# ScalarE makes the convolutions' last tap from TensorE's bank, VectorE adds the other three

## The reference, cut to what matters

```python
def _causal_dwconv(x, w):
    C, K = w.shape
    xt = jnp.transpose(x, (0, 2, 1))
    out = jax.lax.conv_general_dilated(xt, w[:, None, :], window_strides=(1,), padding=[(K - 1, 0)],
                                       feature_group_count=C, dimension_numbers=('NCH', 'OIH', 'NCH'))
    return jnp.transpose(out, (0, 2, 1))
...
q = silu(silu(_causal_dwconv(h @ Wq.T, conv_q)))
k = silu(silu(_causal_dwconv(h @ Wk.T, conv_k)))
v = silu(silu(_causal_dwconv(h @ Wv.T, conv_v)))
q = _l2norm(q.reshape(B, T, nh, hd))
k = _l2norm(k.reshape(B, T, nh, hd))
...
o, memory_state = _delta_scan(k, q, v, beta)
```

## Time and profile before

| what | us |
|---|---|
| median of 3 runs | 1280.63 |
| lowest and highest of them | 1278.09 and 1340.21 |
| the profiled execution's own time | 1278.25 |
| its span, first to last instruction | 1276.4 |
| TensorE busy | 1060.3 (83%) |
| VectorE busy | 944.5 (74%) |
| ScalarE busy | 497.4 (39%) |

### The profile page before, as it was taken

How to read it: one execution, slowest core, us unless ns; L and a number is a source line. 1 busy time by engine, 2 the same in 40 slices (tenths; PEclk the granted TensorE clock), 3 DMA queues, 4 the chain that set the end, 5 groups by cost and what they waited for, 6 DMA issues and landing times.

```text
span 1276.4 us, 22025 instructions
## 1 busy us (share of the span) xinstructions
PE 1060.3 (83%) x8600; PEld 723.6 (57%) x8600; DVE 944.5 (74%) x2425; ACT 497.4 (39%) x1027; POOL 181.4 (14%) x251
## 2 busy tenths in 40 slices
PE   3699778777988999989988998899989889932587
PEld 2356545455556755766566655675566547721465
DVE  3824268897889788987888788977897789779611
ACT  2044254326443644345432653364335443610122
POOL 2000000130122010401040013100040004003100
PEclk9579879978998999989988999999999989975788
DMA  9724023203420143013311242024201300110000
GB/s 288 141 46 72 10 75 76 41 1 100 77 41 1 50 111 63 1 34 95 76 21 33 76 82 35 1 75 101 48 2 32 88 2 1 34 58 0 16 9 9
DMA packets 93608, 67.69 MB, mean 53 GB/s; under 512 B 47233, under 2 KB 86337, under 8 KB 93505
## 3 DMA queue, kind: packets, MB, share of 16 engines
q1 hardware_dynamic: 88544, 60.75, 20.1%
q10 hardware_dynamic: 4960, 5.54, 1.6%
HBM read 45.55 MB, written 20.32 MB: 52 GB/s over the span
## 4 chain that ended last, share of the span: by engine, by line
PE 41%; DVE 37%; ACT 8%; DMA 4%; issue 4%; SPq 4%; POOL 1%; DVEq 0%; ACTq 0%; POOLq 0%
PE bank L1558 7%; DVE lane_buf L1189 5%; PE bank L1509 4%; PE bank L1538 4%; DVE state L1208 4%; PE bank L1712 4%; DVE state L1201 4%; DVE u_l L1196 4%; PE bank L1655 3%; PE bank L1543 3%; PE bank L1504 3%; DVE lane_buf L339 2%; DMA q_l<-lane_q 2%; PE bank L1450 2%; DVE mx L1005 2%
## 5 line engine op out<-in xcount | busy, mean ns | idle before, releaser
L697 ACT ACTIVATE probs<-bank 128x512 f32<-128x512 f32 x256 | 152.1, 597 | 200.1 <-PE bank L1543 199.7
L1558 PE MATMUL bank<-probs,v_ext 128*9 128x128 f32 x2048 | 162.0, 279 | 12.1 <-ACT probs L697 6.7
L1005 DVE TENSOR_REDUCE mx<-bank 128x2 f32<-128x320 f32 x256 | 120.9, 486 | 54.3 <-PE bank L1509 49.4
L1703 PE MATMUL bank<-feat_c,wgu 128*128 128x256 f32 (+1 forms) x384 | 96.3, 402 | 57.2 <-DVE hid_c L1256 51.6
L339 POOL TENSOR_TENSOR lane_buf<-state,q_l 128x128 f32<-128x128 f32 x128 | 86.4, 704 | 353.9 <-DVEq L1214 353.9
L1189 DVE TENSOR_TENSOR lane_buf<-state,til 128x128 f32<-128x128 f32 x256 | 109.6, 428 | 17.1 <-POOL lane_buf L584 10.2
L1703 PEld LDWEIGHTS bank<-feat_c,wgu 128*128 128x128 f32 (+1 forms) x384 | 71.1, 190 | 78.1 <-DVE hid_c L1256 55.7
L1558 PEld LDWEIGHTS bank<-probs,v_ext 128*9 128x9 f32 x2048 | 83.5, 91 | 55.1 <-issue 20.3
L1504 PE MATMUL bank<-edge_mask,identb 128*128 128x64 bf16 x512 | 63.1, 208 | 49.8 <-DVE mx L1005 37.6
L1538 PE MATMUL bank<-tri_mask,identb 128*128 128x512 bf16 x256 | 102.1, 399 | 0.5 <-DMA q_stack<-m_rows 0.5
L1543 PE MATMUL bank<-q_stack,k_stack 128*128 128x128 bf16 x1024 | 101.8, 223 | 0.0
(11 more groups left out here) (167 smaller groups left out, 1766.1 us busy)
## 6 DMA issues: line engine op xcount, KB each, us to landing
k_pieces<-conv SPq DMA_DIRECT2D x48, 128.0 KB, 2.3
k_stack<-k_pieces SPq DMA_DIRECT2D x32, 192.0 KB
k_stack<-k_pieces SPq DMA_DIRECT2D x32, 128.0 KB
k_l<-lane_k SPq DMA_DIRECT2D x8, 512.0 KB, 3.6
q_l<-lane_q SPq DMA_DIRECT2D x8, 512.0 KB, 5.6
q_pieces<-conv SPq DMA_DIRECT2D x24, 128.0 KB, 2.0
q_stack<-q_pieces SPq DMA_DIRECT2D x32, 96.0 KB
tok<-in_x SPq DMA_DIRECT2D x8, 256.0 KB, 3.2
```

What stands on the lines that cost most here:

```text
L697: act.activation(probs[:, u % 2], score_bank[u % 2][:], ACT.Exp, scale=float(DK) ** -0.5).then_inc(exp_done, 1)
L1005: dve.tensor_reduce(mx[:, g, 2 * v:2 * v + 2], bank[1 + u % 2][:, 0:2 * SPAN].rearrange("p (h k) -> p h k", h=2), AX.X, ALU.max).then_inc( ...
L1558: last = pe.matmul(bank[5][row:row + VE, col:col + W], v_ext[:, b, kb, h, :], probs[:, u % 2, (hp * 2 + kb) * W:(hp * 2 + kb + 1) * W], st ...
L1703: last = pe.matmul(late_bank[i % 2][0:m, g * BT:(g + 1) * BT], wgu[:, k, g * INTER + 128 * i:g * INTER + 128 * i + m], fc[:, k], start=(k ...
```

## The change

`raw_of` on ScalarE first writes the last tap's product into conv, straight from TensorE's bank, as a copy with conv_w's column as its scale, in two halves. Then it copies the bank into raw as before. VectorE's `convolve` starts from that: three multiply-adds for taps 0 to 2, and no multiply. The wait for pieces_out moves from VectorE to ScalarE, which now writes conv first. `keep_taps` gets a wait for VectorE's own last multiply-add, which reads the columns that it overwrites.

```diff
--- before.py
+++ after.py
@@ -759,8 +759,14 @@
                 act.wait_ge(projb_done, n * 4 + 1)
                 act.activation(beta_l[:], bank[4][:, 0:W], ACT.Exp, scale=-1.0).then_inc(beta_exp, 1)
 
-            def raw_of(n, s):
+            def raw_of(n, s, front):
                 act.wait_ge(projb_done, n * 4 + s + 2)
+                if front and s == 0:
+
+                    act.wait_ge(pieces_out, n * 144 + 288)
+                for hh in range(HH):
+                    act.activation(conv[:, s, hh * BT:(hh + 1) * BT], bank[1 + s][:, hh * BT:(hh + 1) * BT], ACT.Copy,
+                                   scale=conv_w[:, s, hh, TAPS - 1:TAPS])
                 for hh in range(HH):
                     last = act.copy(raw[:, s, hh, :, TAPS - 1:],
                                     bank[1 + s][:, hh * BT:(hh + 1) * BT].rearrange("p (b t) -> p b t", b=B))
@@ -860,14 +866,14 @@
                 if tail:
                     norm_c(s)
                 if following:
-                    raw_of(n, 0)
-                    raw_of(n, 1)
+                    raw_of(n, 0, front)
+                    raw_of(n, 1, front)
                     if scan:
                         output_squares(t)
                 if front:
                     max_rows(n + 1, 2)
                 if following:
-                    raw_of(n, 2)
+                    raw_of(n, 2, front)
                 def late(i):
                     if tail:
                         relu_c(s, i)
@@ -1067,27 +1073,22 @@
                     dve.wait_ge(tok_c_ready, n * 2 - 3)
                 subtract_scale(x2(n), z(n), mv, rstd, rstd_ready, n * 2 + 2).then_inc(z_ready, 1)
 
-            def convolve(n, s, front):
+            def convolve(n, s):
                 dve.wait_ge(raw_ready, n * 3 + s + 1)
-                if front and s == 0:
-
-                    dve.wait_ge(pieces_out, n * 144 + 288)
-                for tap in range(TAPS):
+                for tap in range(TAPS - 1):
                     for hh in range(HH):
                         src = raw[:, s, hh, :, tap:tap + W]
                         dst = conv[:, s, hh * BT:(hh + 1) * BT].rearrange("p (b t) -> p b t", b=B)
                         w = conv_w[:, s, hh, tap:tap + 1]
-                        if tap == 0:
-                            last = dve.tensor_scalar(dst, src, w, None, ALU.mult)
-                        else:
-                            last = dve.scalar_tensor_tensor(out=dst, in0=src, scalar=w, in1=dst,
-                                                            op0=ALU.mult, op1=ALU.add)
-                    if tap < TAPS - 1:
+                        last = dve.scalar_tensor_tensor(out=dst, in0=src, scalar=w, in1=dst,
+                                                        op0=ALU.mult, op1=ALU.add)
+                    if tap < TAPS - 2:
                         done(last)
                 last.then_inc(conv_ready, 1)
 
-            def keep_taps():
-
+            def keep_taps(n):
+
+                dve.wait_ge(conv_ready, n * 3 + 3)
                 dve.tensor_copy(raw[:, :, :, :, 0:TAPS - 1].rearrange("p s h b t -> p (s h b) t"),
                                 raw[:, :, :, :, W:W + TAPS - 1].rearrange("p s h b t -> p (s h b) t"))
 
@@ -1347,12 +1348,12 @@
                 if tail:
                     third_apply(s)
                 if following:
-                    convolve(n, 0, front)
-                    convolve(n, 1, front)
+                    convolve(n, 0)
+                    convolve(n, 1)
                     if has_scan:
                         output_norm(t)
-                    convolve(n, 2, front)
-                    keep_taps()
+                    convolve(n, 2)
+                    keep_taps(n)
                 if has_scan:
                     if not following:
                         output_norm(t)
```

## The result

The changed kernel takes 1285.83 us, the median of 20 runs (1279.83 to 1288.5), beside 1278.46 for the kernel before in the same number of runs (1275.27 to 1281.48, but for one of 1340.21 that the comparison, which takes fast runs alone, leaves out). The ratio of the two is 1.005, with a 95% interval of 1.0039 to 1.0061. So it is slower by 5 to 8 us, and that is clear of noise although it is well inside 2%. The forecast was 1288 us, 0.7% slower, in a range of 1278 to 1297.

What follows compares the result with a forecast made beforehand. The chain lies mostly on TensorE and VectorE, but ScalarE's way to feat_c decides. Five full bodies 7.2, n = 7 0.8, n = 0 0.6, n = 1 0.3: 8.9 us over 1278.25 is 1287.2, set to 1288 for the runs' median; range 1278 to 1297.

Steps and rivals of the forecast that it cites:

- VectorE's saved work gives nothing: In n = 2 to 7 the 17.5 us VectorE loses lie beside ScalarE's chain, only widening 1.2 us of slack.
- Price of a scaled copy: ScalarE's 48 added copies from a bank: 0.36 us apart, so 0.72 us for two in each of three groups.
- the 20 to 23 that I named as a sign: Sign of being right: ScalarE's busy time over the whole kernel rises by 20 to 23 us.
- The DMA issue holds ScalarE: Max rows' DMA issue before the third group: ScalarE does nothing else meanwhile, so that group starts at 567.47, not 566.75.
- the rival in which the copies are half hidden: If the DMA issue doesn't hold ScalarE, a full body pays 0.72 us only once: 1283.6 us; chance 0.12.
- Full body's stage, 1.44 us: From the k projection to the late FFN's first tile: second and third groups each add 0.72 us.
- the 1.4 named as a sign: Sign of being right: the late FFN's weight load (L1726) waits for feat_c about 1.4 us longer.
- n = 7 was taken at 0.8: Body n = 7, without a DMA issue: second group adds some 0.05, third counts in full: 0.8 us.
- n = 0 was taken at 0.6 and n = 1 at 0.3: Bodies whose ScalarE waited for VectorE: slower by 0.6 us (0.4 to 1.1) and 0.3 us (-0.4 to +0.9).
- The 1.44 us is carried to the l2 norms, the lane DMAs and the next attention: Behind the late FFN's first tile ScalarE's chain passes the delay on: five full bodies make 7.2 us.
- bodies that keep their length as a sign of being wrong: Sign of being wrong: full bodies keep some 137 us or grow by 0.7 only.
- TensorE's clock as the case of the other side: Hole of some 1.4 us before L1726 lowers TensorE's clock in seven bodies: 12.6 us more, 1299.8; chance 0.06.

Runs made afterwards that it cites:

- the first pair of profiles: One profiled execution each of the kernel before (1278.25 us) and the changed kernel, whose span was 8.1 us longer.
- the second pair: Both kernels profiled once more, unaltered: one execution each, 1289.2 us for the changed kernel and 1277.15 for the one before.
- the copies without the saving: Changed kernel with VectorE doing all four taps again, its first multiply overwriting ScalarE's scaled copies: 1285.72 us, ratio 1.0051 to the kernel before.
- the tap for q alone: Changed kernel with ScalarE's scaled copies only for q; k and v keep VectorE's four taps: 1279.1 us, ratio 1.0006 to the kernel before.
- The late-issue kernel: Changed kernel with ScalarE's issue of the max rows' DMA moved to the body's end: 1282.33 us, ratio 1.0043 to the kernel before.
- the copies made twice: Changed kernel with each scaled copy made a second time, into a free part of hid: 1303.81 us, ratio 1.0196 to the kernel before.
- the saving alone: Last tap's product left out: ScalarE as before, VectorE three multiply-adds as in the changed kernel: 1277.14 us, ratio 0.9991 to the kernel before.

## Why the prediction was right, and where it missed

**VectorE's saved work gives nothing: right.** It was the first step, and two experiments bear it out, by giving the work back and by taking it alone.

**Price of a scaled copy: right.** I took 0.36 us from start to start by the Relu row; it is 0.365 (0.73 for two). ScalarE's busy time rose by 16.0 us, less than the 20 to 23 that I named as a sign, since the 20.2 us of the new line overlap with their neighbours. By the figure that I set beside it from the Trainium skill (ScalarE: Activation LUTs, "What ACT_TABLE_LOAD costs"), 0.40, each group would be 0.07 longer. The page's duration for one such copy, 280 + 0.833 x 256 = 493 ns as an estimate, stands against 472 measured here; the measurement decides.

**The DMA issue holds ScalarE: right.** It rested on 0.04 us between two rows in three bodies, against the releaser that the profile names. In the changed kernel the profile still writes "[0.80 <-PE bank L1656]" at 568.84, though TensorE had been done for 0.8 us, and taking the issue away brought the group back behind TensorE. So the rival in which the copies are half hidden falls.

**Full body's stage, 1.44 us: right,** 1.45 to 1.47. The weight load's wait grew by 1.20, not by the 1.4 named as a sign, as 0.25 us of the delay reaches TensorE before that wait. n = 7 was taken at 0.8. Its third pair of evictions starts 0.80 us behind TensorE's last projection where it was 0.04, so 0.76; TensorE itself was 0.45 us quicker in that body, at another clock, and so only 0.35 shows at the units. n = 0 was taken at 0.6 and n = 1 at 0.3; the profile has 0.37 and 0.74, but TensorE's projections took 0.15 less and 0.57 more there than in the profile before, so these two are settled to half a microsecond only.

**"The 1.44 us is carried to the l2 norms, the lane DMAs and the next attention": right to there, and wrong as a sum of bodies.** This is the step that failed: I let a full body grow by what its stage grows, and so put what TensorE's clock does behind the stage at nothing. The short full bodies of the changed kernel are 136.8 to 137.0 us, against 136.5 to 136.9 before, so they grow by 0.4 at most; the long ones, of 139.5 to 139.8, grow by 2.7 to 3.3. I named bodies that keep their length as a sign of being wrong, and half of the four did. In the first pair of profiles the five full bodies grew by 0.0, 2.7, 3.3, 0.4 and 1.2 us, 7.5 in all where 7.2 was forecast; in the second pair they grew by 4.8. That the sum came out so near is luck.

Where the 1.45 us goes is seen at two places that I followed through the bodies. The last exponential of the attention starts 77.6 to 77.7 us into the body in the kernel before and at 79.1 after (79.4 in n = 4), still 1.5 apart. The output projection of the attention (wo_a) starts at 86.8 to 87.7 before and at 87.2 after (87.5 in n = 4). Between them the time is 8.1 us in each of the bodies n = 2 to 5 of both profiles of the changed kernel, and 9.2 to 10.1 in those of the kernel before. The windows over that place, three bodies of before (n = 2, 3, 4) and two of the changed kernel (n = 2, 3):

```profile
504.00:516.00 12.00, 10.51 (x86) 7.38 (x86) 9.87 (x30) 2.38 (x8) 2.23 (x4) 0.72 0.24 43
640.90:652.90 12.00, 10.41 (x86) 7.25 (x86) 9.70 (x30) 2.47 (x8) 2.06 (x4) 0.72 0.25 40
777.70:789.70 12.00, 9.66 (x91) 6.71 (x92) 9.57 (x30) 3.04 (x9) 1.99 (x4) 0.86 0.25 41
```

```profile
505.40:517.40 12.00, 9.66 (x122) 6.53 (x114) 10.45 (x33) 3.86 (x10) 1.58 (x3) 1.00 0.30 52
642.20:654.20 12.00, 9.70 (x125) 6.56 (x117) 10.41 (x33) 3.83 (x10) 1.55 (x3) 1.00 0.30 53
...
661.20:669.20 8.00, 7.32 (x22) 5.63 (x22) 7.38 (x21) 1.92 (x4) 6.96 (x10) 0.57 0.00 0
```

The kernel before has a stretch at 1.2 GHz there in each of its full bodies (0.72 and 0.86 as a mean over 12 us), the changed one has none (1.00): it gets 1.1 to 2.0 us back. Its long body n = 3 has a stretch in another place, 99 us into the body, where the first FFN starts (0.57 over 8 us), and from wo_a to the body's end it takes 52.3 us where the short ones take 49.6 to 49.8: the 2.7. All seven long bodies in the profiles of the kernel before, the changed one, the copies without the saving and the tap for q alone have a stretch of 6.8 us at that place, 99.0 to 99.5 us into the body, and no short one has; the one in n = 4 of the kernel before's second profile is this:

```profile
794.50:802.50 8.00, 7.33 (x23) 5.63 (x22) 7.38 (x20) 1.91 (x4) 7.48 (x11) 0.57 0.00 0
```

The late-issue kernel fits in between. Its stage is 0.7 us longer than before's. In n = 2 it has a short low stretch at the attention's end, as before, 9.3 us there, and the body is 0.7 us longer than before's with such a stretch; in n = 3 it has none, 8.1 us, and the body is 1.0 shorter than that. So a delay of the stage is carried to the end of the body where the clock's pattern stays as it was, and what the prediction lacked is that the pattern moves. In the changed kernel 1.45 less 1.1 is the 0.3 to 0.4 by which its short bodies exceed the 136.6 of before's with the short stretch.

The forecast lies 2.2 us above the measured median, of which 0.8 is what it put on top of its sum; the sum, 8.9, lies 1.5 above the 7.4 between the medians. TensorE's clock moves single bodies by more than that both ways, so it is the likely place of the difference; the medians of runs without a profile can't show it. Why the stretch leaves the attention's end when the stage before it is 1.45 us longer is open, and so is what decides that a body is a long one. The 20 runs of the changed kernel scatter over 8.7 us; body lengths that switch between two values some 2.7 us apart would account for much of it, but only the profiled runs show bodies.

**TensorE's clock as the case of the other side: not here, but real.** I put it behind the hole ahead of the late FFN. At the changed kernel's hole the clock stays at 2.4 GHz; with the copies made twice it falls there in the full bodies, at a price of 0.4 to 0.6 us each, less than half of the 6 us that this kernel loses beyond the copies. The case had the right mechanism in the wrong place: the clock did move the time of whole bodies, but at the attention's end and at the start of the first FFN, and down as well as up.

## What to carry to other kernels

Before moving work from a busy engine to an idle one, find the stretch in which the idle engine would do it and ask what stands behind it in its queue: here ScalarE is busy for 39% of the span, and in the three microseconds that matter it had not a tenth of a microsecond to spare. A DMA issue is work of the engine that issues it, 0.72 us on ScalarE, and a named releaser can hide it: look whether the waiting instruction starts with the issue's end. And count a delay at the end of the body as well as behind the step, since TensorE's clock can give back or add more than the step cost.

## What the runs showed of the hardware that I had not expected

The length of a full body takes two values some 2.7 us apart, 136.9 and 139.5 (once 139.8), with the granted clock 0.99 and 0.96 in the changed kernel, and the same program switches between them from body to body and from run to run.

VectorE's instructions on conv took up to twice their time while GpSimd was at work. The first multiply of the q convolution takes up to 814 ns in the kernel before, with a median of 348; in the kernel with the saving alone a multiply-add takes its place, and the longest is 945 where the median is 481. In both, GpSimd is adding b_dn to x (L566) at that time: the ten multiplies of the kernel before that overlap it take 450 to 814 ns and the other 38 at most 354, and with the saving alone ten multiply-adds take 579 to 945 and the rest at most 489. In the changed kernel, where VectorE starts 0.7 us later, five overlap it, at 533 to 544, and the rest take at most 486. The lines of the first two, durations as least, median and most in ns:

```profile
L1081 DVE TENSOR_SCALAR conv<-raw,conv_w x48: 344/348/814, 164.8 to 1105.2; 128x256 f32<-128x256 f32 x48
```

```profile
L1080 DVE SCALAR_TENSOR_TENSOR conv<-raw,conv_w,conv x144: 476/481/945, 164.8 to 1104.2; 128x256 f32<-128x256 f32 x144
```

That both stretch because of GpSimd is argued from the timelines; no run took GpSimd's work away.
